# A layered sequence model on one core: the second layer's output with tokens on the partitions, states spread four at a time, gate matmuls later

## What is computed

```python
ctx = causal_ema(x, tau_ctx)
wg = sigmoid(concat([x, ctx]) @ Wg.T + bg)
gated = x * wg
h1 = gelu(x @ Wn1.T + bn1)
mod = 0.5 + sigmoid(h1 @ Wn2.T + bn2)                 # 32 traces
traces = [causal_ema(gated * mod[..., d], tau_raws[d]) for d in range(32)]
temporal = einsum('dbtc,dc->btc', traces, softmax(blend, axis=0))
gate = sigmoid(temporal @ Wtemp.T + btemp)
soma = gelu(x @ Wsoma.T + bsoma)
out = (soma * gate) @ Wout.T
return (out - mean(out)) / sqrt(var(out) + 1e-5) * gamma + beta
```

## Time and profile before

| | |
|---|---|
| median of 3 runs | 2221.18 us (2219.94 to 2221.75) |
| profiled execution, span from first to last instruction | 2220.5 us |
| its time against the median | -0.03%; no other time of it is listed |
| granted TensorE clock, mean | 0.974 |
| TensorE busy | 2051.3 us, 92% of the span |
| VectorE busy | 1699.0 us, 77% |
| ScalarE busy | 1196.2 us, 54% |
| GpSimd busy | 796.4 us, 36% |
| second layer, 990 to 1686 us | TensorE busy 654.1, VectorE 559.5, ScalarE 368.7, GpSimd 254.0 us, clock 1.00 |

### The profile page before, as it was taken

One profiled execution on the slowest core, in us unless ns is written; L12 is line 12 of the kernel. 1 busy time (PEld: TensorE's weight loads), 2 busy tenths in 40 slices (PEclk: granted clock), 3 DMA queues, 4 the chain that ended last, 5 costly groups with the idle time before them and its releaser, 6 DMA issues. The chain is left out here.

```text
span 2220.5 us, 42789 instructions
## 1 busy us (share of the span) xinstructions
PE 2051.3 (92%) x14158; PEld 1652.1 (74%) x14158; DVE 1699.0 (77%) x2530; ACT 1196.2 (54%) x2428; POOL 796.4 (36%) x589
## 2 busy tenths in 40 slices
PE   3899999999999999759999999999995999999998
PEld 2566666666666666447777777777774999999997
DVE  6788888888888888577878888887875566666664
ACT  2466565666665666435555555555554555555553
POOL 4645444444455554033333333333340111111111
PEclk8999999999999999879999999999997999999998
DMA  3444444444444444100000000000001222222221
GB/s 92 106 106 107 107 110 110 108 109 108 105 105 106 108 109 104 24 25 1 0 0 0 0 0 0 0 0 0 0 0 59 78 79 70 85 69 80 85 66 60
DMA packets 121171, 137.47 MB, mean 62 GB/s; under 512 B 24240, under 2 KB 89776, under 8 KB 121136
## 3 DMA queue, kind: packets, MB, share of 16 engines
q1 hardware_dynamic: 118576, 128.64, 22.9%
q0 software_dynamic: 2560, 8.39, 1.0%
HBM read 48.35 MB, written 8.39 MB: 26 GB/s over the span
## 5 line engine op out<-in xcount | busy, mean ns | idle before, releaser
L366 DVE TENSOR_REDUCE a_neg_max<-a_s 128x2 f32<-128x512 f32 x512 | 329.1, 683 | 123.4 <-PE a_s L613 121.8
L487 ACT ACTIVATE a_e<-a_t 128x512 f32<-128x512 f32 x512 | 281.2, 610 | 228.4 <-PE a_t L626 228.4
L375 DVE SCALAR_TENSOR_TENSOR a_e<-a_e,a_w_t 128x1024 f32<-128x1024 f32 x256 | 373.6, 1469 | 4.1 <-ACT a_e L487 4.1
L613 PE MATMUL a_s<-a_k_st,a_q_st 96*128 96x256 f32 x1024 | 275.4, 380 | 0.0
L613 PEld LDWEIGHTS a_s<-a_k_st,a_q_st 96*128 96x128 f32 x1024 | 203.5, 199 | 13.7
L610 PE MATMUL a_s<-a_add_m,ident_bf 128*128 128x512 bf16 x512 | 201.8, 394 | 7.9 <-POOL a_add_m L254 5.8
L1695 ACT ACTIVATE c_hid<-c_pH,c_b 128x256 f32<-128x256 f32 x256 | 107.4, 471 | 186.3 <-PE c_pH L1758 185.9
L897 POOL TENSOR_TENSOR b_decayed<-b_table,b_mod_t 128x1024 f32<-128x1024 f32 x64 | 118.6, 1872 | 210.3 <-ACT b_mod_t L1163 203.0
L1317 PE MATMUL b_pS<-b_gated_t,b_decayed 128*128 128x256 f32 x768 | 189.5, 390 | 0.7
L626 PE MATMUL a_t<-a_q_st,a_k_st 97*128 97x512 f32 x512 | 177.1, 426 | 2.6 <-DMA a_q_st<-a_max_row 2.0
L642 PE MATMUL a_v<-a_e,a_v_pad 128*32 128x256 f32 x2048 | 163.6, 392 | 4.5 <-DVE a_e L375 2.1
(11 more groups left out here) (261 smaller groups left out, 5720.4 us busy)
## 6 DMA issues: line engine op xcount, KB each, us to landing
a_q_st<-a_q_hi SPq DMA_DIRECT2D x256, 128.0 KB, 2.4
a_k_st<-a_k_hi SPq DMA_DIRECT2D x256, 64.0 KB, 2.0
a_q_st<-a_q_lo SPq DMA_DIRECT2D x128, 128.0 KB, 2.4
a_xs<-in_xT SPq DMA_DIRECT2D x32, 256.0 KB, 2.8
a_k_st<-a_k_lo SPq DMA_DIRECT2D x128, 64.0 KB, 2.1
x_all<-in_xT SPq DMA_DIRECT2D x32, 256.0 KB, 2.8
c_we<-in_we SPq DMA_DIRECT2D x32, 256.0 KB, 2.7
c_key_t<-in_keyT SPq DMA_DIRECT2D x32, 256.0 KB, 3.2
```

Source lines behind the costliest of these rows:

```text
L366: dve.tensor_reduce(neg_max[:, qc, head:head + 2], ps_s[b][:], AX.X, ALU.max, negate=True).then_inc(red_done, 1)
L375: dve.scalar_tensor_tensor(out=buf[:], in0=buf[:], scalar=BIG, in1=w_t[par][:, kc].unsqueeze(1).to_broadcast([P, 4, S]), op0=ALU.min, op1= ...
L487: act.activation(e[g % E_BUFS][:, 2 * b:2 * b + 2], ps_t[b][:], ACT.Exp).then_inc(exp_done, 1)
L613: ins = pe.matmul(ps_s[b][:, r], q_st[par][0:96, slot, qc * P:qc * P + P], k_st[par][0:96, slot // 2], start=False, stop=(r == 1))
```

## The change

- `output` exchanges its operands: `mixed` is stationary and `Wout` moving, so that tokens lie on the partitions and channels in the free direction.
- The variance is a sum over the free direction. ScalarE makes it while squaring, in two instructions of 256 columns with `accum_out`; `mean_square` and its matrix are gone. The square root and VectorE's reciprocal work on 128x2 (`deviation`, `inverse`).
- ScalarE multiplies with the reciprocal (`normalized`, two instructions), TensorE turns the result back with four transposes into `pB` (`turn_normed`), and `scaling` reads `pB`.
- `state` has four buffers in place of two; `spread` is called twice a lap with four matmuls each, in place of four times with two.
- TensorE's order: `hidden` and the first `gate_in` stand in front of `gate_out`; the states calls 2 and 3 both stand in front of `output`; `turn_normed` stands behind the `lags` call 6. VectorE's order follows. On ScalarE `normalized` stands behind `input_gate`.

```diff
-    state = [sb(f"state{i}", [P, 2, D]) for i in range(2)]
+    state = [sb(f"state{i}", [P, 2, D]) for i in range(4)]
-    square = sb("square", [P, C, S])
-    std = sb("std", [P, S])
-    rstd = sb("rstd", [P, S])
-    normed = sb("normed", [P, C, S])
-    scaled = sb("scaled", [P, C, S])
+    square = sb("square", [P, D])
+    var = sb("var", [P, C])
+    std = sb("std", [P, C])
+    rstd = sb("rstd", [P, C])
+    normed = wtemp
+    scaled = wsoma
...
         def states(n, q):
             dve.wait_ge(st_done, 4 * n + q + 1)
-            if not (isinstance(n, int) and n == 0 and q < 2):
-                dve.wait_ge(yin_done, 4 * n + q - 1)
-            dve.tensor_tensor(state[q % 2][:], pS[q % 2][:], ...
+            if not (isinstance(n, int) and n == 0):
+                dve.wait_ge(yin_done, 2 * n - 1 + q // 2)
+            dve.tensor_tensor(state[q][:], pS[q % 2][:], ...
...
-        def norm(n):
+        def inverse(n):
             dve.wait_ge(std_done, n + 1)
             at_least(dve, normed_done, n)
             dve.reciprocal(rstd[:], std[:]).then_inc(rstd_done, 1)
-            dve.wait_ge(rstd_done, n + 1)
-            at_least(dve, scaled_done, n)
-            dve.tensor_tensor(normed[:], pZ[:], rstd[:].unsqueeze(1).to_broadcast([P, C, S]), ALU.mult).then_inc(normed_done, 1)
...
-        def squares(n):
+        def deviation(n):
             act.wait_ge(out_mm, n + 1)
-            at_least(act, var_mm, n)
-            act.activation(square[:], pZ[:], ACT.Square).then_inc(sq_done, 1)
-        def deviation(n):
-            act.wait_ge(var_mm, n + 1)
+            for m in range(C):
+                act.activation(square[:], pZ[:, m], ACT.Square, accum_out=var[:, m:m + 1]).then_inc(sq_done, 1)
+                act.wait_ge(sq_done, C * n + m + 1)
             at_least(act, rstd_done, n)
-            act.activation(std[:], pB[:, 0], ACT.Sqrt, bias=eps[:]).then_inc(std_done, 1)
+            act.activation(std[:], var[:], ACT.Sqrt, bias=eps[:], scale=1.0 / D).then_inc(std_done, 1)
             act.activation(table_pick[:], eps[:], ACT.Gelu)
+        def normalized(n):
+            act.wait_ge(rstd_done, n + 1)
+            at_least(act, back_done, n)
+            for m in range(C):
+                ins = act.activation(normed[:, m], pZ[:, m], ACT.Copy, scale=rstd[:, m:m + 1])
+            ins.then_inc(normed_done, 1)
         def scaling(n):
-            act.wait_ge(normed_done, n + 1)
+            act.wait_ge(back_done, n + 1)
...
-        def spread(n, q):
-            pe.wait_ge(sw_done, 4 * n + q + 1)
-            if q == 0:
+        def spread(n, h):
+            pe.wait_ge(sw_done, 4 * n + 2 * h + 2)
+            if h == 0:
                 at_least(pe, tho_done, n)
-            for i in range(2):
-                j = (2 * q + i) % 4
-                ins = pe.matmul(pY[32 * j:32 * j + 32, q // 2], spread_w[:], state[q % 2][:, i],
+            for j in range(4):
+                ins = pe.matmul(pY[32 * j:32 * j + 32, h], spread_w[:], state[2 * h + j // 2][:, j % 2],
...
-                ins = product(pZ[:, m], wout_p, mixed_p, [(k, k) for k in range(C)], m)
+                ins = product(pZ[:, m], mixed_p, wout_p, [(k, k) for k in range(C)], m)
...
-        def mean_square(n):
+        def turn_normed(n):
             pe.wait_ge(tht_done, NB if isinstance(n, int) and n + 3 > NB else n + 3)
-            pe.wait_ge(sq_done, n + 1)
-            for k in range(C):
-                ins = pe.matmul(pB[:, 0], mean_mat[:], square[:, k], start=(k == 0), stop=(k == C - 1))
-            ins.then_inc(var_mm, 1)
+            pe.wait_ge(normed_done, n + 1)
+            for m in range(C):
+                for c in range(C):
+                    ins = pe.transpose(pB[:, c, m * P:m * P + P], normed[:, m, c * P:c * P + P], ident[:])
+            ins.then_inc(back_done, 1)
```

More of the change, by code:

```diff
@@ L796, in trace_layer @@
     mean_w = sb("mean_w", [P, C])
-    mean_mat = sb("mean_mat", [P, P])
     eps = sb("eps", [P, 1])
@@ L843, in trace_layer @@
     soma_mm, soma_done, gate_mm, tho_done, mixed_done = (sem(n) for n in ("soma_mm", "soma", "gate_mm", "tho", "mixed"))
-    out_mm, sq_done, var_mm, std_done, rstd_done, normed_done, scaled_done, x2_done = (
-        sem(n) for n in ("out_mm", "sq", "var_mm", "std", "rstd", "normed", "scaled", "x2"))
+    out_mm, sq_done, std_done, rstd_done, normed_done, back_done, scaled_done, x2_done = (
+        sem(n) for n in ("out_mm", "sq", "std", "rstd", "normed", "back", "scaled", "x2"))
     TABLES = {"tau_c": tau_c, "tau_col": tau_col, "tau_row": tau_row, "blend_t": blend_t, "lag_n": lag_n, "ramp": ramp,
@@ L942, in _ @@
         link(dve.memset(eps[:], 1e-5))
-        link(dve.memset(mean_mat[:], 1.0 / D))
+        link(dve.memset(var[:], 0.0))
         for tau in (tau_c, tau_col, tau_row):
@@ L1066, in body @@
             lag_sum(n, par, 0)
+            lag_sum(n, par, 1)
             if has_c:
                 mixing(n - 1)
-            lag_sum(n, par, 1)
+            lag_sum(n, par, 2)
+            lag_sum(n, par, 3)
+            states(n, 2)
             if has_c:
                 low_mixed(n - 1)
-            lag_sum(n, par, 2)
-            lag_sum(n, par, 3)
+            states(n, 3)
             if has_a:
                 modulation(n + 1, 1 - par)
-            states(n, 2)
             lag_sum(n, par, 4)
+            lag_sum(n, par, 5)
             if has_c:
-                norm(n - 1)
-            states(n, 3)
-            lag_sum(n, par, 5)
+                inverse(n - 1)
             if has_a:
@@ L1093, in _ @@
         low_mixed(NB - 1)
-        norm(NB - 1)
+        inverse(NB - 1)
     @block.scalar
@@ L1226, in body @@
             if has_c:
-                squares(n - 1)
                 deviation(n - 1)
@@ L1231, in body @@
             if has_c:
+                normalized(n - 1)
                 scaling(n - 1)
@@ L1248, in _ @@
         high_mixed(NB - 1)
-        squares(NB - 1)
         deviation(NB - 1)
+        normalized(NB - 1)
         scaling(NB - 1)
@@ L1379, in body @@
             states(n, par, 1)
+            if has_a:
+                hidden(n + 1, 1 - par)
+                gate_in(n + 1, 1 - par, 0)
             if has_c:
                 gate_out(n - 1)
-            if has_a:
-                hidden(n + 1, 1 - par)
             lags(n, par, 2)
-            if has_a:
-                gate_in(n + 1, 1 - par, 0)
             spread(n, 0)
@@ L1390, in body @@
                 modulate_rows(n + 1)
+            states(n, par, 2)
+            states(n, par, 3)
             if has_c:
@@ L1394, in body @@
                 modulate_cols(n + 1)
-            spread(n, 1)
-            states(n, par, 2)
-            if has_c:
-                mean_square(n - 1)
             lags(n, par, 4)
@@ L1402, in body @@
             lags(n, par, 5)
-            states(n, par, 3)
-            spread(n, 2)
+            spread(n, 1)
             lags(n, par, 6)
-            spread(n, 3)
+            if has_c:
+                turn_normed(n - 1)
             lags(n, par, 7)
@@ L1425, in _ @@
         output(NB - 1)
-        mean_square(NB - 1)
+        turn_normed(NB - 1)
 HIDDEN = 1024
```

8 lines of the change are left out of this document (4 added, 4 removed).

## The result

| | before | after |
|---|---|---|
| median | 2221.47 us (4 runs, 2219.94 to 2221.82) | 2365.22 us (4 runs, 2362.03 to 2367.99) |
| ratio, 95% interval | | 1.0651 [1.0636, 1.0666] |
| span of the profiled execution | 2220.5 us | 2363.0 us |
| granted TensorE clock, mean | 0.974 | 0.936 |
| lap of the second layer, mean of the 31 between `total` of batch 0 and of batch 31 | 22.25 us | 26.74 us |

The change makes the kernel 6.5% slower. The forecast was 2340 us in a range of 2280 to 2395. The laps explain almost all of it: 31 x (26.74 - 22.25) = 139.2 of the 142.5 us between the two spans.

What follows compares the result with a forecast made beforehand. TensorE was taken as the bound, with one 1.33 us hole a lap. The lap's chain rises from 22.31 to 25.01 us: 2220.5 + 81 - 4 = about 2298, plus 42 for the clock gives 2340 us, range 2280 to 2395.

Steps and rivals of the forecast that it cites:

- the prediction's list: Lap from turn_back: to ctx_lo; second gate_in half; gate_out to spread; spread through modulate_rows; states; output; ScalarE to normed; transposes through turn.
- The three waits: New TensorE waits per lap: gate_in for ctx_lo 1.3 us, spread(0) for th_o 0.9, turn_normed's transposes for normed 3.1.
- ScalarE's way: ScalarE's chain from the start of modulate_cols to normed: 6.65 us, against 3.55 of TensorE work meanwhile.
- 1.4 a lap: Clock term: half-speed stretches after the new stall cost 1.4 us in each lap, 42 us in all.
- gain some 4: Batch 0, batch 31 without th_g, and the tail without the big reciprocal together gain some 4 us.
- 0.56 for a call of four, a saving of 1.12: TensorE's spread: two calls of four at 0.56 us replace four calls of two, saving 1.12 us a lap.
- VectorE's relief is worth nothing by itself: VectorE's smaller reciprocal (1.74 us before) gains nothing, since VectorE ends last only at temp_lo, whose queue place is unchanged.
- the rows name ScalarE's own instructions back to back: Argument against the faster rival: ScalarE's own instructions fill the chain to normed, so relieving VectorE would not shorten it.
- The clock holds: Rival: slower by the chain alone, with TensorE's clock staying up in the laps: 2298 us; chance 0.25.
- The drain after a table load: Rival: the skill's 1.38 us drain follows each ScalarE table load: 2381 us, more with the clock; chance 0.02.
- waits 1 and 2: TensorE waits in front of spread: gate_in's second half for ctx_lo, 1.3 us; spread(0) for th_o, 0.9.
- Faster: Rival: ScalarE's chain to normed fits TensorE's 3.55 us, lap 21.91, 2204 us (about 2170 without waits 1 and 2); chance 0.05.

Runs made afterwards that it cites:

- e2: The changed kernel with gate_out put back in front of hidden and the first gate_in: 2300.39 us.
- e3: The changed kernel with the first gate_in cut around gate_out, the x half ahead and the context half behind: 2270.30 us.
- e4: The kernel before with only four state buffers and the spread in two calls of four: 2218.13 us, ratio 0.9987.
- g2: The kernel before with the spread of four, and VectorE's norm and state of call 3 moved between product and sum of lag_sum 4: 2197.12 us.
- e5: The changed kernel without square root, both table loads and reciprocal; VectorE passes the variance on instead: 2337.34 us.
- e1: The changed kernel with 24 matmuls of 256 columns added just before turn_normed's wait: 2310.09 us.
- f3: The changed kernel reordered: gate_in split, output and modulate_cols between states 2 and 3, turn_normed behind lags 7, normalized, low_mixed and inverse earlier: 2207.82 us.
- g1: The reordered changed kernel (f3) with VectorE's modulation ahead of its state of call 3 and inverse behind lag_sum 4: 2154.75 us.

## Why the prediction was right, and where it was not

- **The chain.** Forecast 25.01 us a lap at full clock; the one full lap at full clock has 24.79. Its parts in the order of the prediction's list, forecast and measured: 5.85 and 5.89, 0.72 and 0.82, 2.71 and 2.61, 1.15 and 1.35, 3.66 and 3.27, 1.61 and 1.62, 6.65 and 6.66, 2.66 and 2.57. Only the states were off by much. The three waits were forecast at 1.3, 0.9 and 3.1 and came out at 1.30 (1.03 at full clock), 0.79 and 3.16. That ScalarE's way came so near is in part luck: the squares took 0.98 (forecast 1.14), the root 0.31 to the next load (0.2), and the pair of `normed` 0.98 until TensorE started (0.9), and these errors cancel. TensorE's cover was 3.51 (3.55).
- **The clock.** The mechanism was right: a stall of 3 us in each lap, half clock behind it. The term "1.4 a lap" was mis-sized: it measured 2.16. It was made from a low stretch of 3.8 us. A mean clock of 0.89 in laps of 26.74 means some 5.9 us at half speed in each, an estimate that takes the two levels 1.2 and 2.4 GHz only. e2 and e3 show that it can't be priced by one stall: with the same 3.16 us for `normed`, but with less idle time ahead of it, the clock in the laps is 0.94 and 0.93.
- **The sum.** The forecast was 23 us under the span of 2363.0. A full lap was forecast at 25.01 + 1.4 = 26.41 and lasts 26.95, which makes 30 x 0.54 = 16: the clock was 0.76 too small, the chain 0.22 too long, and in part they cancelled. The edges make the other 7 or so: "gain some 4" was forecast, and the spans differ by some 2.5 more than the full laps do. From the last `total` to the layer's last `scaling` it is 16.1 us after the change and 15.4 before, a loss where the prediction saw a gain without the big reciprocal. Behind the layer the span is 2.8 longer, which is less than executions of the changed kernel differ by (2362.03 to 2367.99).
- **The spread.** "0.56 for a call of four, a saving of 1.12": 0.57 measured, and TensorE's busy time fell by 1.26 a lap in e4. What the text did not say is that this gain, made alone, would be worth nothing until VectorE's queue is reordered (e4 and g2).
- **"VectorE's relief is worth nothing by itself", "the rows name ScalarE's own instructions back to back".** The first does not hold in the changed kernel: with the old reciprocal of 1.74 alone, VectorE's way to `normed` would have ended at about 1262.6 (1261.03 + 1.59, an estimate), behind the 1261.40 at which `normalized` starts. The second is true of ScalarE and hid a second chain: VectorE's way ended 0.37 us before ScalarE's. It was relieved of 1.74 + 0.69 and at the same time loaded with 2.65 by GpSimd's decays. VectorE's sums had been taken at the lengths of a lap in which the decays hardly ran beside them. The forecast was not harmed, since ScalarE still ended last, but e5 was: I expected a lap of 22.7, 4 us shorter, and got 0.77.
- **The rivals.** "The clock holds" (2298) fell; e1, which holds the clock by added matmuls, comes to 2310. The drain after a table load fell: the instruction behind starts 0.01 to 0.02 us later, and the measurement decides. The text's "about 2170" without waits 1 and 2 does not follow from its terms: 21.91 - 1.3 - 0.9 = 19.71 a lap would give 2138. "Faster" (2204) needed ScalarE's chain under 3.95; it had 6.67. f3 and g1 show that the faster side was to be had, by other orders, not by a shorter chain: g1 runs both loads, both 1.28 long, in each lap.

## What to carry to other kernels

When a step is moved to fill a hole, ask of each of its halves when its own input is there; a step that can be cut often fills the hole where the whole only moves it. When a chain is shortened, look for the second one that ends almost as late, and re-read the durations of everything that now runs at another time: an operation's length belongs to its place as well. And a new wait on the engine that bounds the kernel is paid twice if the clock falls behind it.

## What the hardware showed that was not expected

**VectorE and GpSimd shut each other out for whole instructions, where both work on SBUF.** In the changed kernel the decays are two instructions (mean ns of one over the laps, 2385 and 1450):

```profile
L897 POOL TENSOR_TENSOR b_decayed<-b_table,b_mod_t 128x1024 f32<-128x1024 f32 x18 | 42.9, 2385 | 197.4 <-ACT b_mod_t L1160 197.4
...
L897 POOL TENSOR_TENSOR b_decayed<-b_table,b_mod_t 128x512 f32<-128x512 f32 x18 | 26.1, 1450 | 0.0
```

The first runs from 1256.95 to about 1259.33. VectorE's sum, started at 1257.14, ends at 1259.62, which is the end of that instruction plus 0.29. The next sum starts at 1260.00, and ends at 1260.95, 0.21 after the decays end at 1260.74. In f3 the two modulation steps end at 1250.19 and 1251.47, where the decays change over at about 1250.04 (1247.66 + 2.38) and end at 1251.33. It hits sums of two SBUF tiles and the modulation steps, which read and write SBUF. Products with a PSUM operand are spared (0.34 at 1259.54, in the middle of the decays). It was there before the change too, in both directions, GpSimd's residual first, VectorE's sum second:

```profile
1238.53 1.81 POOL L903 TENSOR_TENSOR x_all<-b_scaled,x_all 128x512 f32 x1 [3.98 <-ACT b_scaled L1206]
```

```profile
1239.52 0.97 DVE L1028 TENSOR_TENSOR b_inner<-b_inner,b_prod 128x128 f32<-128x128 f32 x1
```

VectorE's gating (two SBUF inputs) had started at 1238.50, 0.03 ahead of the residual, and took its usual 0.68; the residual took 1.81, where it takes 1.28 undisturbed. The sum had to wait for the residual's end at 1240.34 and ended 0.15 later.

The Trainium skill ("SBUF — State Buffer", section "SBUF: two separate sides") states this: a shared pair of ports is an exclusive lock and not a split of bandwidth, and whichever instruction starts first holds it to its end. On VectorE's side it names operations in a two-port mode, and those with two SBUF inputs, the latter only against a GpSimd instruction that reads SBUF. The numbers above agree for the sums, the gating and the residual. The modulation steps have one SBUF input; that they run in a two-port mode no run here shows. It is the rule that would have told of the second chain, and the prediction left it out. In the lap before only one sum was caught for long.

**The accumulated sum has an instruction of its own.** `accum_out` adds an ACTIVATION_READ_ACCUMULATOR of 0.19 us to each square, which starts 0.26 to 0.28 after the square does; the two squares together still took 0.98.
